# A Mamba block on one core: the seam columns of u*B move from GpSimd to VectorE and ScalarE

## The chip, the cores and the metric

The kernel runs on one core of a Trainium2 chip. The metric is the device time of one execution in microseconds. TensorE is called PE, VectorE DVE, ScalarE ACT, GpSimd POOL and SyncE SP, as the profile does.

## The reference, cut to what matters

The input has 2 sequences of 2048 rows and 512 columns. A layer norm with modulation stands ahead of a Mamba mixer (1024 channels, 16 states a channel), and a second layer norm with modulation ahead of one dense layer that stands for the sum of 8 factors; each branch is gated and added to the input. The change is in the mixer's recurrence, which is elementwise over channels and states and sequential over rows:

```
dA  = exp(dt[..., None] * A)
dBu = (dt * h)[..., None] * Bp[:, :, None, :]
s   = s * dA_t + dBu_t            # one step for each of the 2048 rows
y   = einsum('lben,bln->ble', states, Cp) + h * D
```

In the kernel's names, `u` is dt*h, `ub` is u*B, `decay` is dA, and the product of the states with C is summed over the 16 states by PE.

## The kernel before, in words

All data is fp32. Rows are taken in 16 chunks of 256 rows, 8 for each sequence. The 1024 channels are 8 tiles of 128 partitions, taken as 4 pairs. A **unit** is one of the 16 states for one pair of tiles: 128 partitions by 2*256 columns. So a chunk has 64 units. A **quad** is 4 units (16 quads in a chunk, 4 for each pair of tiles), a **step** is 2 units (32 in a chunk, called s).

For each unit, ACT writes the decays (an exp, two instructions of 256 and 255 columns, `decays`, L722) into one of three PSUM banks. DVE scans them with `ub` (L1426): a unit's 512 columns are scanned in one instruction, although its two halves belong to two tiles. The scan of the first half must not run on into the second, so the decay at the seam (the first column of the second half) is zero (ACT writes that zero, L718, where the product with C overwrote it), and the state that the second tile carries in from the chunk before is added to `ub` in that one column instead. The value that is added is seam = exp(decay rate * dt of the row) * carried state, 128 x 4 for a quad. Chunks 0 and 8 begin a sequence and have no such value; the other 14 do, and are called seamed here.

POOL makes `ub` for a quad at a time (`make_ub`, L568: 128 x 2048 columns out of `u` and `b_all`), two quads ahead of the scans, in a ring of three. In a seamed chunk it then waits for its own product and adds 4 seam values to it (L582); twice a chunk it multiplies the exps (made by ACT, `seam_decays`, L845) with the carried states (`make_seam`, L554).

The states are multiplied with C in one of two places. For each quad a table (`EVEN_POOL`, `ODD_POOL` for chunks 2 to 14, by their parity) says how many of its 4 units, the last ones, go to POOL: DVE scans these into `state_p` in SBUF and POOL multiplies them in one instruction (`multiply_c`, L596, 128 x 512 or 128 x 1024 columns). The other units stay in their PSUM bank, and DVE multiplies them into `sc_d` (L1441). After that, ACT copies the last column to `carry` (`keep_carry`, L706). PE turns every product by a matmul with the identity and sums it in one bank (L1010).

Beside this, every chunk has other work, put at written-out steps on every engine: projections, taps and gates of the neighbouring chunks on PE; `taps` (L1481), `silu_before`, `silu_gate`, residual sums and statistics on DVE; modulation, tanh, copies and softplus on ACT; `u` (L545) and two small norm steps on POOL. Every engine works its own list in order, and semaphores tie the lists together. POOL's order at quad q is: make `ub` of quad q+2 (which waits for the scans of quad q-1), then the product with C of quad q (which waits for the scans of quad q and for the carry copy of its last unit), then `u` at quads 0, 2, 3 and 13. SP's list holds the loads; the load of B for a chunk waits for the last quads of `ub` of the chunk before.

Where data lies matters for the rows below. `decay`, `bank_a`, `bank_c` and `y_bank` are PSUM banks; `ub`, `u`, `b_all`, `c_all`, `state_p`, `sc_d`, `seam`, `carry`, `hc`, `dt`, `yg`, `xc`, `bias_row` and the rest are in SBUF. A scan has one tensor input in PSUM (the decays) and one in SBUF (`ub`), and so has DVE's product with C.

Of the kernel before, what the change touches and what calls it, by code (L numbers as in the profile page):

```python
# [22 lines left out]
ALU = mybir.AluOpType  # L23
# [12 lines left out]
PAIRS = KE // 2  # L36
UNITS = N * PAIRS
# [20 lines left out]
EVEN_POOL = (2, 2, 2, 2, 2, 2, 2, 2, 2, 2, 2, 1, 1, 1, 1, 1)  # L58
ODD_POOL = (2, 2, 2, 2, 1, 2, 2, 2, 2, 2, 2, 1, 1, 1, 1, 1)
# [17 lines left out]
NORMS = 2 + LB  # L77

# [38 lines left out]
def seam_count(c):  # L117

    return c - c // PER

# [44 lines left out]
def build(nc, x, win_m, xp_t, dt_t, wo_t, chan, cond_t, wmod, factors, bias, out):  # L165
# [11 lines left out]
    with ExitStack() as ctx:  # L177
# [83 lines left out]
        ub_product, seam_decay, seam_made, seam_zeroed = sem("ub_product"), sem("seam_decay"), sem("seam_made"), sem("seam_zeroed")  # L261
# [60 lines left out]
        def _(sp):  # L322
# [10 lines left out]
            def load_b(c, par, h):  # L333

                if c:
                    sp.wait_ge(ub_made, QUADS * c - 2 * (1 - h) - 1)
                sp.wait_ge(bc_stored, 16 * c + 16)
# [175 lines left out]
        def _(pool):  # L513
# [33 lines left out]
            def make_seam(c, half):  # L547

                qs = slice(2 * half, 2 * half + 2)
                pool.wait_ge(seam_decay, 2 * seam_count(c) - 1 + half)  # L550
                pool.wait_ge(carried, carries_after(UNITS * (c - 1) + N * qs.stop - 1))
                odd = carry[c // PER][:, :, :].rearrange("p n (q j) -> p n q j", j=2)[:, :, qs, 1]
                part = seam[c % 2][:, :, qs]
                pool.tensor_tensor(part, part, odd, ALU.mult).then_inc(seam_made, 1)  # L554

            def make_ub(quad):
# [7 lines left out]
                if q == 0 and n % (N // 2) == 0 or quad == 1:  # L564
# [6 lines left out]
                                   ALU.mult).then_inc(ub_product if c % PER else ub_made, 1)  # L571
                if c % PER == 0:
                    return
                if g == 0:
                    make_seam(c, 0)
                    pool.wait_ge(seam_made, 2 * seam_count(c) - 1)
                if g == 4:
                    make_seam(c, 1)
                    pool.wait_ge(seam_made, 2 * seam_count(c))
                pool.wait_ge(ub_product, QUADS * (seam_count(c) - 1) + g + 1)  # L580
                first = ub[:, slot, :, 1, 0]
                pool.tensor_tensor(first, first, seam[c % 2][:, n:n + QUAD, q], ALU.add).then_inc(ub_made, 1)  # L582
# [107 lines left out]
        def _(act):  # L690
# [146 lines left out]

            def seam_decays(c, par, half):
# [78 lines left out]
            def one_round(c, par, la, lc):  # L917
                for s in range(STEPS):
# [22 lines left out]
                    if c == 0 and s in (7, 12):  # L941
                        rows_absolute(s // 12, (0.5, RANK ** -0.5)[s // 12])
# [787 lines left out]
```

## Time and profile before

| | |
|---|---|
| median of 3 runs | 2019.82 us (2019.42 to 2027.12) |
| the profiled execution | 2025.55 us, its span 2023.8 us |
| PE matmul | 1759.7 us busy, 87% of the span |
| DVE | 1867.4 us, 92% |
| ACT | 1517.1 us, 75% |
| POOL | 1835.7 us, 91% |
| mean granted PE clock | 0.973 |

How to read it: the busy time is what an engine's own instructions took, the time an instruction needed to get at its operands included, but not the time for which it was held back by a semaphore. The span is some microseconds short of the device time. The chain that ended last passes through PE (42% of the span), ACT (19%), POOL (15%) and DVE (13%).

### The profile page before, as it was taken

To read this page: it belongs to the slowest core of one execution; us is meant where nothing else is said; L and a number is where in the kernel's file an instruction comes from. 1 tells how busy PE (TensorE), PEld (TensorE's weight loads), DVE (VectorE), ACT (ScalarE), POOL (GpSimd) and SP (SyncE) were. 2 spreads that over 40 slices of the span, in tenths; PEclk is the share of its full clock that TensorE was granted. 3 is DMA by queue.
4 is the path that set the end of the run, shared out by engine and by line. 5 is a ranking of instruction groups with operands and counts; after the bars stand their busy time and mean duration, and the time that the engine had idled before them with its cause. 6 is when DMAs were issued, how large, how long until landed. Compare 5 with 4: busy or idle time off the path is not lost.

```text
span 2023.8 us, 29343 instructions
## 1 busy us (share of the span) xinstructions
PE 1759.7 (87%) x9128; PEld 1312.2 (65%) x9128; DVE 1867.4 (92%) x2240; ACT 1517.1 (75%) x4646; POOL 1835.7 (91%) x925
## 2 busy tenths in 40 slices
PE   7985889889889898988989888898988899898798
PEld 5664757667576765757666675766757576676564
DVE  2799989999999999999999999999999999999995
ACT  3767778697877869777786977878787786878662
POOL 1789999999999999999998999999999999999992
PEclk9897999999999999999999999999999999999798
DMA  4656514132140412304042240403223040311200
GB/s 171 235 114 153 140 48 147 31 121 79 43 143 15 152 47 97 103 30 154 17 141 68 111 141 22 157 22 131 68 73 121 28 156 22 121 53 55 92 27 32
DMA packets 72001, 186.17 MB, mean 92 GB/s; under 512 B 6818, under 2 KB 8482, under 8 KB 63908
## 3 DMA queue, kind: packets, MB, share of 16 engines
q1 hardware_dynamic: 68148, 176.95, 26.3%
q0 software_dynamic: 3696, 7.34, 2.2%
q8 instruction: 73, 1.20, 0.2%
q14 instruction: 84, 0.69, 0.1%
HBM read 172.20 MB, written 12.06 MB: 91 GB/s over the span
## 4 chain that ended last, share of the span: by engine, by line
PE 42%; ACT 19%; POOL 15%; DVE 13%; issue 9%; DMA 1%; DVEq 0%; POOLq 0%; SPq 0%; ACTq 0%
PE y_bank L1010 10%; PE bank_a L1085 10%; PE bank_c L1157 9%; POOL ub L568 8%; ACT decay L722 7%; DVE decay L1426 5%; POOL state_p L596 5%; PE bank_c L1057 4%; DVE state_p L1426 3%; PE bank_a L1068 2%; ACT dt L835 2%; DVE sc_d L1441 2%; ACT L722 2%; ACT hT L737 2%; ACT L835 2%
## 5 line engine op out<-in xcount | busy, mean ns | idle before, releaser
L568 POOL TENSOR_TENSOR ub<-u,b_all 128x2048 f32<-128x2048 f32 x255 | 1160.4, 4551 | 48.5 <-DMA b_all<-bc_scratch 47.4
L722 ACT ACTIVATE decay<-dt,decay_rate 128x256 f32<-128x256 f32 (+1 forms) x2048 | 889.6, 466 | 36.0 <-DVE state_p L1426 34.3
L1426 DVE TENSOR_TENSOR_SCAN decay<-decay,carry,ub 128x512 f32<-128x512 f32 x610 | 763.7, 1277 | 25.8 <-ACT decay L722 23.8
L596 POOL TENSOR_TENSOR state_p<-state_p,c_all 128x1024 f32<-128x1024 f32 (+1 forms) x256 | 498.7, 1948 | 85.3 <-ACT carry L706 82.4
L1426 DVE TENSOR_TENSOR_SCAN state_p<-decay,carry,ub 128x512 f32<-128x512 f32 x414 | 527.4, 1274 | 9.3 <-ACT decay L722 7.2
L1010 PE MATMUL y_bank<-ident,sc_d 128*128 128x128 f32 x2440 | 362.5, 283 | 79.9 <-DVE sc_d L1441 79.5
L1441 DVE TENSOR_TENSOR sc_d<-decay,c_all 128x512 f32<-128x512 f32 x610 | 406.7, 671 | 0.0
L1010 PEld LDWEIGHTS y_bank<-ident,sc_d 128*128 128x128 f32 x2440 | 292.9, 145 | 146.1 <-DVE sc_d L1441 120.8
L706 ACT ACTIVATE carry<-decay 128x2 f32<-128x2 f32 x610 | 100.8, 165 | 264.8 <-DVE sc_d L1441 262.9
L1010 PEld LDWEIGHTS y_bank<-ident,state_p 128*128 128x128 f32 x1656 | 195.7, 143 | 126.9 <-POOL state_p L596 71.7
L1010 PE MATMUL y_bank<-ident,state_p 128*128 128x128 f32 x1656 | 231.0, 279 | 53.2 <-POOL state_p L596 52.0
L1085 PE MATMUL bank_a<-hT,win_h 128*128 128x256 f32 x992 | 240.5, 387 | 32.4 <-DVE hc L1490 30.0
L1057 PE MATMUL bank_c<-hT,win_z 128*128 128x256 f32 x960 | 230.7, 387 | 0.0
L1157 PE MATMUL bank_c<-wo,yg 128*128 128x512 f32 x480 | 223.8, 594 | 0.0
L1085 PEld LDWEIGHTS bank_a<-hT,win_h 128*128 128x128 f32 x992 | 182.3, 193 | 58.7 <-DVE hc L1490 35.7
L1057 PEld LDWEIGHTS bank_c<-hT,win_z 128*128 128x128 f32 x960 | 181.7, 196 | 22.6
L1068 PE MATMUL bank_a<-pre_z,tap_diag 128*128 128x256 f32 x496 | 120.4, 386 | 12.2 <-DVE bank_a L1481 12.2
L1157 PEld LDWEIGHTS bank_c<-wo,yg 128*128 128x128 f32 x480 | 86.6, 191 | 67.0 <-issue 64.8
L1068 PEld LDWEIGHTS bank_a<-pre_z,tap_diag 128*128 128x128 f32 x496 | 92.7, 191 | 39.8 <-DVE bank_a L1481 15.8
L1187 PE MATMUL bank_c<-ffn,hT 128*128 128x512 f32 x240 | 115.9, 605 | 0.0
L1001 PE MATMUL y_bank<-ident,skipped 128*128 128x128 f32 x256 | 42.9, 294 | 71.5 <-ACT y_rows L811 71.5
L718 ACT ACTIVATE decay<-ident 128x1 f32<-128x1 f32 x608 | 103.4, 170 | 0.1
(139 smaller groups left out, 1842.1 us busy)
## 6 DMA issues: line engine op xcount, KB each, us to landing
win_h<-win_m SPq DMA_DIRECT2D x128, 256.0 KB, 2.6
win_z<-win_m SPq DMA_DIRECT2D x128, 256.0 KB, 2.8
b_all<-bc_scratch SPq DMA_DIRECT2D x31, 1024.0 KB, 4.7
c_all<-bc_scratch SPq DMA_DIRECT2D x31, 1024.0 KB, 6.6
xa<-x SPq DMA_DIRECT2D x16, 512.0 KB, 5.0
xc<-x SPq DMA_DIRECT2D x16, 512.0 KB, 3.8
out<-xc SPq DMA_DIRECT2D x15, 512.0 KB, 4.0
ffn<-factors POOLq DMA_DIRECT2D x7, 1024.0 KB, 10.0
```

The source lines that it names most:

```text
L568: pool.tensor_tensor(ub[:, slot, :, :, :], u[:, (PAIRS * c + q) % U_PAIRS, :, :].unsqueeze(1).to_broadcast([P, QUAD, 2, ROWS]), b_all[:, n ...
L596: pool.tensor_tensor(part, part, c_all[:, n + QUAD - k:n + QUAD, :].unsqueeze(2).to_broadcast([P, k, 2, ROWS]), ALU.mult).then_inc(pooled, 1)
L718: act.activation(bk[:, ROWS:ROWS + 1], ident[:, 0:1], ACT.Copy, scale=0.0)
L722: last = act.activation(bk[:, j * ROWS + j:(j + 1) * ROWS], dt[:, pair % DT_PAIRS, j, j:], ACT.Exp, scale=decay_rate[:, e, n:n + 1])
L1010: last = pe.matmul(y_bank[:, at:at + P], tile[:, j, t * P:(t + 1) * P], ident[:, :], start=False, stop=last_of_pair, is_transpose=True, sk ...
L1057: last = pe.matmul(dst[:, j * ROWS:(j + 1) * ROWS], tile[:, k, :], hTc[:, k, :], start=(k == 0), stop=(k == KD - 1))
L1068: last = pe.matmul(h_lane(c, q)[:, j * ROWS:(j + 1) * ROWS], tap_diag[:, i, 2 * q + j, :], pre[q % 2][:, j, k:k + ROWS], start=False, stop ...
L1085: last = pe.matmul(h_lane(c, q)[:, j * ROWS:(j + 1) * ROWS], win_h[i % H_TILES][:, k, :], hT[c % H_RING][:, k, :], start=(k == 0 and j == ...
L1157: last = pe.matmul(bank_c[t][:, :], yg[:, k, t * P:(t + 1) * P], wo[:, k, :], start=(k == 0), stop=(k == KE - 1))
L1187: last = pe.matmul(bank_c[t][:, :], hT[c % H_RING][:, k, t * P:(t + 1) * P], ffn[:, k, :], start=False, stop=(k == KD - 1))
L1426: dve.tensor_tensor_scan(dst, bk[:, :], ub[:, quad % UB_RING, i, :, :].rearrange("p j r -> p (j r)"), carried_in[:, n, 2 * q:2 * q + 1], A ...
L1441: dve.tensor_tensor(sc_d[:, i % D_RING, :, :], bk[:, :].rearrange("p (j r) -> p j r", j=2), c_all[:, n:n + 1, :].to_broadcast([P, 2, ROWS] ...
```

## The change

Four parts; the first three concern the 14 seamed chunks:

- POOL no longer touches the seam: `make_seam`, the wait for its own product and the small sum L582 go. `make_ub` raises `ub_made` at once.
- DVE makes the whole seam column ahead. `carry_seam` (two a chunk, 128 x 32 columns) does what `make_seam` did. `add_to_seam` (five a chunk, 128 x 16 or 128 x 8 columns) adds u*B of the seam's row to it, from `b_all`, `u` (as the per-partition scalar) and `seam`. In the chunk's own steps they stand at s = 1, 4, 5, 12 and 20, and for the next chunk at s = 28 and 29, each behind `scan(unit)` and ahead of `scan(unit + 1)` of that step.
- ACT copies 4 values from `seam` over the column in `ub` (`add_seam`, 16 a chunk), ahead of the decays of each quad's first unit; it waits for `ub_made` and `seam_added`. DVE's scan of a quad's first unit waits for that copy (`ub_seamed`). On ACT `tanh_gate` moves ahead of other work of its step at s = 1, 3, 5.
- The tables: in chunks 2 to 14 quads 11 and 13 give two products to POOL instead of one, quad 7 gives one instead of two, and in the odd ones quad 4 gives two instead of one. POOL then has 28 products in each of these chunks, against 27 (even) and 26 (odd). SP's load of B also waits for `seam_added`.

```diff
-EVEN_POOL = (2, 2, 2, 2, 2, 2, 2, 2, 2, 2, 2, 1, 1, 1, 1, 1)
-ODD_POOL = (2, 2, 2, 2, 1, 2, 2, 2, 2, 2, 2, 1, 1, 1, 1, 1)
+EVEN_POOL = (2, 2, 2, 2, 2, 2, 2, 1, 2, 2, 2, 2, 1, 2, 1, 1)
+ODD_POOL = (2, 2, 2, 2, 2, 2, 2, 1, 2, 2, 2, 2, 1, 2, 1, 1)
...
+SEAM_ADDS = PAIRS + 1
...
                 if c:
                     sp.wait_ge(ub_made, QUADS * c - 2 * (1 - h) - 1)
+                    wait(sp, seam_added, SEAM_ADDS * seam_count(c - 1))
...
-            def make_seam(c, half):
...
-                                   ALU.mult).then_inc(ub_product if c % PER else ub_made, 1)
-                if c % PER == 0:
-                    return
-                if g == 0:
-                    make_seam(c, 0)
-                    pool.wait_ge(seam_made, 2 * seam_count(c) - 1)
-                if g == 4:
-                    make_seam(c, 1)
-                    pool.wait_ge(seam_made, 2 * seam_count(c))
-                pool.wait_ge(ub_product, QUADS * (seam_count(c) - 1) + g + 1)
-                first = ub[:, slot, :, 1, 0]
-                pool.tensor_tensor(first, first, seam[c % 2][:, n:n + QUAD, q], ALU.add).then_inc(ub_made, 1)
+                                   ALU.mult).then_inc(ub_made, 1)
...
+            def add_seam(quad):
+
+                c, g = quad // QUADS, quad % QUADS
+                q, n = QUAD * g // N, QUAD * g % N
+                act.wait_ge(ub_made, quad)
+                act.wait_ge(seam_added, SEAM_ADDS * (seam_count(c) - 1) + (q + 1 if q or n >= N // 2 else 0) + 1)
+                act.activation(ub[:, quad % UB_RING, :, 1, 0], seam[c % 2][:, n:n + QUAD, q], ACT.Copy).then_inc(ub_seamed, 1)
...
+                    if c % PER and s % 2 == 0:
+                        add_seam(step // 2)
                     decays(2 * step)
...
+                elif i == 0 and quad // QUADS % PER:
+                    dve.wait_ge(ub_seamed, seamed_count(quad))
...
+            def carry_seam(c, half):
+
+                qs = slice(2 * half, 2 * half + 2)
+                dve.wait_ge(seam_decay, 2 * seam_count(c) - 1 + half)
+                dve.wait_ge(carried, carries_after(UNITS * (c - 1) + N * qs.stop - 1))
+                odd = carry[c // PER][:, :, :].rearrange("p n (q j) -> p n q j", j=2)[:, :, qs, 1]
+                part = seam[c % 2][:, :, qs]
+                dve.tensor_tensor(part, part, odd, ALU.mult).then_inc(seam_made, 1)
+
+            def add_to_seam(c, q, half=None):
+
+                pair = PAIRS * c + q
+                ns = slice(0, N) if half is None else slice(half * N // 2, (half + 1) * N // 2)
+                dve.wait_ge(u_made, pair)
+                dve.wait_ge(seam_made, 2 * seam_count(c) - 1 + q // 2)
+                if q == 0:
+                    dve.wait_ge(b_loaded[half], 16 * c + 16)
+                part = seam[c % 2][:, ns, q]
+                dve.scalar_tensor_tensor(out=part, in0=b_all[:, ns, 0], scalar=u[:, pair % U_PAIRS, 1, 0:1], in1=part,
+                                         op0=ALU.mult, op1=ALU.add).then_inc(seam_added, 1)
...
+                    if c % PER and s == 1:
+                        add_to_seam(c, 0, 1)
+                    if c % PER and s == 4:
+                        carry_seam(c, 1)
+                    if c % PER and s in (5, 12, 20):
+                        add_to_seam(c, {5: 1, 12: 2, 20: 3}[s])
+                    if la is not None and (c + 1) % PER and s == 28:
+                        carry_seam(c + 1, 0)
+                    if la is not None and (c + 1) % PER and s == 29:
+                        add_to_seam(c + 1, 0, 0)
                     scan(unit + 1)
```

## Rows read from the trace of the kernel before

**Rows 1.** The page: busy us, share of the span and instructions of each engine.

```profile
PE 1759.7 (87%) x9128; PEld 1312.2 (65%) x9128; DVE 1867.4 (92%) x2240; ACT 1517.1 (75%) x4646; POOL 1835.7 (91%) x925
```

**Rows 2.** Windows, one stretch of a chunk's length: PE, PEld, DVE, ACT, POOL, clock, DMA.

```profile
600.00:720.00 120.00, 106.37 (x566) 80.30 (x565) 114.55 (x138) 93.96 (x288) 115.34 (x59) 0.99 0.26 84
```

**Rows 3.** Groups by form: line, engine, out<-in, count | busy us, mean ns | idle before.

```profile
L568 POOL TENSOR_TENSOR ub<-u,b_all 128x2048 f32<-128x2048 f32 x255 | 1160.4, 4551 | 48.5 <-DMA b_all<-bc_scratch 47.4
...
L1441 DVE TENSOR_TENSOR sc_d<-decay,c_all 128x512 f32<-128x512 f32 x610 | 406.7, 671 | 0.0
L596 POOL TENSOR_TENSOR state_p<-state_p,c_all 128x1024 f32<-128x1024 f32 x158 | 372.8, 2359 | 66.4 <-ACT carry L706 63.5 <-DVE decay L1426 2.7
...
L596 POOL TENSOR_TENSOR state_p<-state_p,c_all 128x512 f32<-128x512 f32 x98 | 126.0, 1285 | 18.9 <-ACT carry L706 18.9
...
L582 POOL TENSOR_TENSOR ub<-ub,seam 128x4 f32<-128x4 f32 x224 | 46.8, 209 | 17.6
...
L706 ACT ACTIVATE carry<-state_p 128x4 f32<-128x4 f32 x158 | 30.8, 195 | 0.5 <-DVE state_p L1426 0.5
```

**Rows 4.** The same view, DVE alone: its operations whose two tensor inputs are in SBUF.

```profile
L1544 DVE SCALAR_TENSOR_TENSOR bias_row<-bias_row,dt 2x512 f32<-2x512 f32 x1 | 10.3, 10256 | 0.0
...
L1573 DVE TENSOR_TENSOR u<-dt,hc 128x512 f32<-128x512 f32 x1 | 0.7, 693 | 7.1 <-ACT dt L835 7.1
...
L1584 DVE SCALAR_TENSOR_TENSOR cond_s<-cond_s,cond 128x8 f32<-128x8 f32 x1 | 0.2, 168 | 3.6 <-ACT cond_s L898 3.6
```

**Rows 5.** Timeline around L1544 (POOL and DVE): start us, us, engine, operation.

```profile
145.64 2.83 POOL L618 TENSOR_TENSOR wo<-wo,y_rows 128x1024 f32<-128x1024 f32 x1
...
146.73 10.26 DVE L1544 SCALAR_TENSOR_TENSOR bias_row<-bias_row,dt 2x512 f32<-2x512 f32 x1
...
147.96 4.96 POOL L568 TENSOR_TENSOR ub<-u,b_all 128x2048 f32<-128x2048 f32 x1
152.43 1.71 POOL L596 TENSOR_TENSOR state_p<-state_p,c_all 128x512 f32<-128x512 f32 x1
153.65 2.78 POOL L611 TENSOR_TENSOR hT<-wo,y_rows 128x1024 f32<-128x1024 f32 x1
...
156.51 2.68 POOL L618 TENSOR_TENSOR wo<-wo,y_rows 128x1024 f32<-128x1024 f32 x1
156.91 1.27 DVE L1426 TENSOR_TENSOR_SCAN decay<-decay,carry,ub 128x512 f32<-128x512 f32 x1
```

**Rows 6.** Timeline, POOL then DVE, around step 4 of chunk 4.

```profile
575.93 4.54 POOL L568 TENSOR_TENSOR ub<-u,b_all 128x2048 f32<-128x2048 f32 x1
...
580.70 2.36 POOL L596 TENSOR_TENSOR state_p<-state_p,c_all 128x1024 f32<-128x1024 f32 x1
583.00 4.55 POOL L568 TENSOR_TENSOR ub<-u,b_all 128x2048 f32<-128x2048 f32 x1
...
577.43 2.46 DVE L1426 TENSOR_TENSOR_SCAN decay<-decay,carry,ub 128x512 f32<-128x512 f32 x2
```

**Rows 7.** Timeline, POOL then DVE, steps 1 and 2 of chunk 4.

```profile
566.68 4.53 POOL L568 TENSOR_TENSOR ub<-u,b_all 128x2048 f32<-128x2048 f32 x1
...
572.37 2.36 POOL L596 TENSOR_TENSOR state_p<-state_p,c_all 128x1024 f32<-128x1024 f32 x1 [0.87 <-ACT carry L706]
...
568.98 1.27 DVE L1426 TENSOR_TENSOR_SCAN state_p<-decay,carry,ub 128x512 f32<-128x512 f32 x1
...
570.75 2.65 DVE L1426 TENSOR_TENSOR_SCAN decay<-decay,carry,ub 128x512 f32<-128x512 f32 x2
```

**Rows 8.** Timeline, POOL then DVE, around step 28 of chunk 4.

```profile
670.00 1.27 POOL L596 TENSOR_TENSOR state_p<-state_p,c_all 128x512 f32<-128x512 f32 x1
671.23 1.28 POOL L545 TENSOR_TENSOR u<-dt,hc 128x512 f32<-128x512 f32 x1
672.59 4.54 POOL L568 TENSOR_TENSOR ub<-u,b_all 128x2048 f32<-128x2048 f32 x1
...
669.51 1.28 DVE L1426 TENSOR_TENSOR_SCAN decay<-decay,carry,ub 128x512 f32<-128x512 f32 x1
```

More of the change, by code:

```diff
@@ L119, in seam_count, with seamed_count @@
     return c - c // PER
+def seamed_count(quad):
+    c, g = quad // QUADS, quad % QUADS
+    return QUADS * (seam_count(c) - 1) + g + 1
 def products_after(unit):
@@ L260, in build @@
         skip_turned, y_copied = sem("skip_turned"), sem("y_copied")
-        ub_product, seam_decay, seam_made, seam_zeroed = sem("ub_product"), sem("seam_decay"), sem("seam_made"), sem("seam_zeroed")
+        ub_seamed, seam_decay, seam_made, seam_zeroed = sem("ub_seamed"), sem("seam_decay"), sem("seam_made"), sem("seam_zeroed")
+        seam_added = sem("seam_added")
         a_full = [sem(f"a_full{i}") for i in range(2)]
@@ L545, in make_u @@
                 pool.tensor_tensor(u[:, pair % U_PAIRS, :, :], dt[:, pair % DT_PAIRS, :, :], hc[:, k, :], ALU.mult).then_inc(u_made, 1)
-            def make_seam(c, half):
[L549 to L554, printed above, removed]
             def make_ub(quad):
@@ L836, in soft_dt @@
                 last.then_inc(dt_made, 1)
+            def add_seam(quad):
+                c, g = quad // QUADS, quad % QUADS
+                q, n = QUAD * g // N, QUAD * g % N
+                act.wait_ge(ub_made, quad)
+                act.wait_ge(seam_added, SEAM_ADDS * (seam_count(c) - 1) + (q + 1 if q or n >= N // 2 else 0) + 1)
+                act.activation(ub[:, quad % UB_RING, :, 1, 0], seam[c % 2][:, n:n + QUAD, q], ACT.Copy).then_inc(ub_seamed, 1)
             def seam_decays(c, par, half):
                 act.wait_ge(dt_made, PAIRS * c + 2 * half + 2)
-                wait(act, ub_made, QUADS * (c - 1) - 1)
+                wait(act, ub_seamed, QUADS * seam_count(c - 2))
                 for q in (2 * half, 2 * half + 1):
@@ L942, in one_round @@
                         rows_absolute(s // 12, (0.5, RANK ** -0.5)[s // 12])
+                    if lc is not None and s in (1, 3, 5):
+                        tanh_gate(c - 1, {1: 1, 3: 2, 5: 3}[s])
                     if s in (4, 6, 12):
@@ L962, in one_round @@
                     if lc is not None:
-                        if s in (1, 3, 5):
-                            tanh_gate(c - 1, {1: 1, 3: 2, 5: 3}[s])
                         if s == 21:
```

## The prediction, made before the changed kernel was run

> **What bounds the kernel now.** I read the page first: DVE is busy for 1867 us and POOL for 1836 us of the span, ACT for 1517 us [rows 1]. Then the windows, to see whether that is an average over unlike stages. It is not: one stretch of 120 us in the middle has DVE at 114.6 us and POOL at 115.3 us, ACT at 94 us and PE at 106 us at almost its full clock [rows 2]. DVE has 5.4 us in such a stretch in which it is not busy. So DVE is the engine that hardly ever rests, POOL is close behind, and any time that DVE loses beyond 5.4 us a chunk is lost to the kernel. Next the groups by form, for prices: a product with C takes DVE 0.671 us and POOL 1.29 us for one unit or 2.36 us for two, a quad of `ub` takes POOL 4.55 us, the seam sum 0.209 us, and a carry copy of 4 columns takes ACT 0.195 us [rows 3].
>
> **What a small operation on DVE costs.** The change puts 7 of them into each of 14 chunks, 98 in all: 2 `carry_seam` and 5 `add_to_seam`. By width they should be cheap: one of 8 columns took 0.168 us [rows 4]. But they differ from DVE's daily work in one thing. Scans and products with C have one tensor input in PSUM; each of the seven has both in SBUF. So I looked for DVE operations of that kind in the trace. There are three. Two took 0.168 and 0.693 us, as their widths ask, and both ran before POOL began its first `ub`. The third, L1544, 512 columns wide like the one of 0.693 us, took 10.256 us [rows 4].
>
> The timeline shows what it did in that time: nothing, as long as POOL ran [rows 5]. It starts at 146.73, when POOL is in L618. POOL goes on through `ub`, a product and L611, its instructions following each other without a hole. L611 ends at 156.43, the next POOL instruction waits for L611's own result and starts at 156.51, and in this hole of 0.08 us DVE gets in: it ends at 156.99, 0.56 us after L611, its plain duration. POOL's next instruction is 0.3 us longer than others of 1024 columns (2.68 against 2.36 us [rows 3, 5]). So a DVE operation with two SBUF inputs is shut out while POOL runs, and once shut out it waited through three of POOL's instruction boundaries. It is one case, but one of one.
>
> The Trainium skill, SBUF — State Buffer, section Who interferes with whom, has the rule: a DVE instruction with two SBUF inputs contends with a GpSimd instruction that reads SBUF, whoever starts first has the shared ports for its whole instruction, and the other fully blocks. The trace agrees that DVE blocks; it goes further than the rule in that three boundaries passed.
>
> **The sum of the stalls.** DVE works in order, so scans and products queue behind the shut-out instruction, and ACT's decays, which wait for freed banks, behind these. What ends a stall is POOL running dry: at quad q it makes `ub` of quad q+2 and then needs the scans of quad q, which DVE now withholds. So a stall lasts from the insertion to the end of `ub` of quad q+2, unless POOL has a hole earlier.
> - Step 4 (quad 2). Chunk 4 starts that quad's first two scans at 577.43 and the operation would stand between them, at about 578.66. POOL starts the product of quad 1 at 580.70 and ends `ub` of quad 4 at 587.55 [rows 6]. As it stands that is 8.9 us. But stalls let POOL catch up. The least that it can lag is seen where it waited for the carry copy: product at 572.37, first scan of the next quad at 570.75, a lag of 1.62 us [rows 7], in place of 3.27. Then the stall is 1.62 + 6.85 (product to end of `ub`) - 1.23 = 7.2 us. I take the least lag, since the stalls recur. The operation of step 5 finds POOL waiting and costs nothing.
> - Steps 12 and 20 (quads 6 and 10) have the same pattern: 7.2 us each, 8.9 at most.
> - Step 1: DVE is at 568.98, POOL in a `ub` until 571.21 and then without work: 2.2 us [rows 7].
> - Step 28: DVE is at 669.51; POOL has the product of quad 13 ahead, which the new table makes 1.1 us longer, and then `u`, ending at 672.51. The `ub` behind needs that `u`, and there is a hole of 0.08 us [rows 8]. So 3.0 + 1.1 = 4.1 us. Step 29 costs 0 to 1 us.
>
> Together 21.6 + 2.2 + 4.1 = 28 us a chunk, 34 with POOL's present lag. The 5.4 us that DVE now waits [rows 2] partly vanish, since during a stall PE and ACT catch up; I take 4. That leaves 24 us a chunk and, for 14 chunks, 336 us. The last value is an estimate; the bound below is a stall of nothing but the operation itself (98 times 0.17 = 17 us), and I take the blocked value because it is the row of the same kind of operands that decides.
>
> **The other terms.** DVE loses 19 products with C (7 even chunks with one, 6 odd with two): 19 * 0.67 = 13 us less, against 17 us for the seven operations' own time. POOL loses 224 sums and 28 products of the seam, each with a wait of its own, and gains 19 products of 1.07 us each; it will be the one that waits, so this is worth nothing. ACT gets 224 copies of 0.195 us [rows 3], 3.1 us a chunk, and has 26 us free [rows 2], more when DVE is late; nothing. `add_seam` waits for POOL's `ub` ahead of the decays. At quad 4 of chunk 4 that `ub` ends at 587.55 and POOL is to be ahead of the scans more than now, so this wait is nothing while DVE is late. Moving `tanh_gate` is worth tenths of a microsecond. SP's added wait is for additions of the chunk before, long done. So the rest sums to about zero.
>
> The sum is made against the profiled execution: 2025.55 + 336 = 2361. The median lies 5.7 us lower, so the forecast is **2355 us**. With the slack used in full and stalls of 24 us a chunk it is some 2270, with POOL's present lag and 2 us of slack regained some 2470: its own range.
>
> **Rivals.**
> - *Taking turns* (0.18): the shared ports change hands at each boundary, and a stall is only what is left of POOL's current instruction. Speaking for it: L1544 is one case. Against it: L1544 itself. At step 4 DVE would wait from 578.66 for a `ub` that ends at 580.47, 1.8 us [rows 6]; at step 1, 2.2 us [rows 7]; taken as 1.8 us for each of the seven it is 12.6 us, less 4 to 5 of slack, so 7.5 us a chunk: 105 us, **2125 us**. This is what the page's rule gives by its letter (The Trainium skill, SBUF — State Buffer).
> - *No shutting out* (0.12), the other side: operations of 8 to 32 columns slip in, and L1544 was late for another reason, its 2 partitions or its DMA-loaded input. Place: the late quads, 11 and 13, where DVE and ACT are both full. Price: the 19 products with C are gained, at most 13 us, POOL's relief helps in chunk 1, where it has extra work, some 3 us, and the own time is half hidden. That is -8 us, **2012 us**. It decides if a seam operation takes DVE under 0.3 us on average.
> - *ACT becomes the bound* (0.04): shutting out does not occur, and the copies lengthen ACT's full stretches. 5 copies a chunk exposed, at 0.2 to 0.3 us, give 14 * 1.3 = 18 us, **2030 to 2040 us**.
> - *More than blocked* (0.04): the stalls make PE idle, its granted clock falls, and its backlog bounds the chunk: over 2470 us.
> - That the change doesn't do what it says: the added operations are unconditional in the seamed chunks, so I give it no chance of its own.
>
> **How the numbers follow.** Blocked with a long stall 0.62, taking turns 0.18, not shut out 0.12, ACT 0.04, worse 0.04. A measurement of this kernel tells about 0.5% (10 us) from no change. The rival at 2012 is split between within 0.5% and faster by more (0.06 and 0.06); ACT's goes to slower but for 0.01; so faster 0.06, same 0.07, slower 0.87. The range reaches from the take-turns case to near the end of the forecast's own: 2110 to 2450; it leaves out the two cases at no change and the worst end, 2 in 10.
>
> **What would show it.** The new DVE groups, 28 and 70 instructions, should have a mean of several microseconds, with the longest at 7 us and those of steps 5 and 29 near 0.2 us, and 300 to 400 us busy in all; each should end about 0.1 to 0.2 us behind a POOL instruction. DVE's share stays over 90%, as a blocked instruction counts as busy; POOL's falls to about 80% with a wait for `carried` ahead of products; ACT's longest wait is for DVE. If those groups' means are under 0.3 us the forecast is wrong altogether; if they are near 2 us the turns are taken and the step that failed is the one that lets a stall run to POOL's running dry.

## The result, and the profile after

The changed kernel takes 2147.09 us (median of 4 runs, 2138.94 to 2147.9), the kernel before 2019.96 us beside it: a ratio of 1.061 [1.058, 1.065], slower by 127 us. The profiled execution is one of these runs, 2147.07 us with a span of 2145.3 us; its mean granted TensorE clock is 0.953, against 0.973 before. (Of the experiments below, the one with an input from PSUM was profiled in a disturbed execution with a span of 4589.6 us, in which POOL was busy for only 39% of the time, so of its rows only single operations of DVE are read, beside what POOL did at that moment.)

The page's line of busy times and the same 120 us stretch as before, after [rows 1] and [rows 2]:

```profile
PE 1806.1 (84%) x9128; PEld 1331.8 (62%) x9128; DVE 2010.9 (94%) x2319; ACT 1532.0 (71%) x4832; POOL 1806.2 (84%) x673
```

```profile
600.00:720.00 120.00, 104.83 (x551) 77.65 (x549) 116.81 (x136) 89.50 (x281) 104.32 (x37) 0.98 0.25 83
```

The forecast was 2355 us. The change is slower, as forecast, but by 127 us and not by 336.

DVE has 143.5 us more of busy time and the span grew by 121.5 us; so DVE's time without work shrank by only 22 us in all, 1.6 us a seamed chunk. In the stretch POOL fell from 115.3 to 104.3 us and ACT from 94 to 89.5: both now wait. Where DVE's time went stands in its groups by form (line, operation, out<-in, count | busy us, mean ns | idle before):

```profile
L1463 DVE TENSOR_TENSOR sc_d<-decay,c_all 128x512 f32<-128x512 f32 x591 | 391.3, 666 | 0.0
L1449 DVE SCALAR_TENSOR_TENSOR seam<-b_all,u,seam 128x16 f32<-128x16 f32 x42 | 70.9, 1689 | 0.0
...
L1449 DVE SCALAR_TENSOR_TENSOR seam<-b_all,u,seam 128x8 f32<-128x8 f32 x28 | 50.0, 1787 | 0.0
L1438 DVE TENSOR_TENSOR seam<-seam,carry 128x32 f32<-128x32 f32 x28 | 45.1, 1611 | 0.0
```

The 98 new operations are busy for 166.0 us (70.9 + 50.0 + 45.1), 1.7 us each where their widths ask for 0.17. The products with C went from 406.7 us [rows 3] to 391.3, the 19 fewer. The two lines by themselves, with the shortest, the median and the longest duration in ns:

```profile
L1438 DVE TENSOR_TENSOR seam<-seam,carry x28: 477/1650/8768, 184.2 to 2012.6; 128x32 f32<-128x32 f32 x28
```

```profile
L1449 DVE SCALAR_TENSOR_TENSOR seam<-b_all,u,seam x70: 218/1524/3477, 192.4 to 2071.8; 128x16 f32<-128x16 f32 x42, 128x8 f32<-128x8 f32 x28
```

The same operation takes 0.5 or 8.8 us, so the price is not the operation's own. The timeline of chunk 4 shows its seven, at steps 1, 4, 5, 12, 20, 28 and 29 (start us, duration us):

```profile
603.90 0.35 DVE L1449 SCALAR_TENSOR_TENSOR seam<-b_all,u,seam 128x8 f32<-128x8 f32 x1
...
614.64 1.88 DVE L1438 TENSOR_TENSOR seam<-seam,carry 128x32 f32<-128x32 f32 x1
...
619.99 3.32 DVE L1449 SCALAR_TENSOR_TENSOR seam<-b_all,u,seam 128x16 f32<-128x16 f32 x1
...
650.36 0.32 DVE L1449 SCALAR_TENSOR_TENSOR seam<-b_all,u,seam 128x16 f32<-128x16 f32 x1
...
681.22 1.52 DVE L1449 SCALAR_TENSOR_TENSOR seam<-b_all,u,seam 128x16 f32<-128x16 f32 x1
...
710.21 0.50 DVE L1438 TENSOR_TENSOR seam<-seam,carry 128x32 f32<-128x32 f32 x1
...
715.39 3.47 DVE L1449 SCALAR_TENSOR_TENSOR seam<-b_all,u,seam 128x8 f32<-128x8 f32 x1
```

And POOL's timeline in the same stretches:

```profile
611.92 4.54 POOL L568 TENSOR_TENSOR ub<-u,b_all 128x2048 f32<-128x2048 f32 x1
616.42 2.35 POOL L585 TENSOR_TENSOR state_p<-state_p,c_all 128x1024 f32<-128x1024 f32 x1
618.74 4.53 POOL L568 TENSOR_TENSOR ub<-u,b_all 128x2048 f32<-128x2048 f32 x1
...
678.16 4.53 POOL L568 TENSOR_TENSOR ub<-u,b_all 128x2048 f32<-128x2048 f32 x1
...
714.28 4.54 POOL L568 TENSOR_TENSOR ub<-u,b_all 128x2048 f32<-128x2048 f32 x1
```

Step 4's operation starts in a `ub` that ends at 616.46 and ends itself at 616.52. Step 5's ends at 623.31, the `ub` at 623.27; step 20's at 682.74, the `ub` at 682.69; step 29's at 718.86, the `ub` at 718.82. Each ends 0.04 to 0.06 us behind the end of the POOL instruction that was under way when it came, and POOL's next one, though ready (the product at 616.42), does not keep it out. That is a stall of what is left of one instruction. The two timelines read in full say the same of nearly all: 95 of the 98 end 0.02 to 0.06 us behind the end of the one POOL instruction under way, and in 42 of these POOL's next instruction followed without a hole. Two more found POOL without work (231.40 and 2043.93) and took 0.23 and 0.22 us. Over the 14 seamed chunks the mean is 0.47 us at step 1, 2.28 at step 4, 3.11 at step 5, 0.37 at step 12, 1.59 at step 20, 0.94 at step 28 and 3.10 at step 29, 11.9 us a chunk.

There is one exception, step 4 of chunk 1. DVE, then POOL (the first of POOL's rows lies ahead of the stall):

```profile
219.15 8.77 DVE L1438 TENSOR_TENSOR seam<-seam,carry 128x32 f32<-128x32 f32 x1
```

```profile
215.25 1.29 POOL L592 DMA_DIRECT2D ffn<-factors  x1
216.07 5.04 POOL L568 TENSOR_TENSOR ub<-u,b_all 128x2048 f32<-128x2048 f32 x1
220.57 2.84 POOL L585 TENSOR_TENSOR state_p<-state_p,c_all 128x1024 f32<-128x1024 f32 x1
222.88 4.97 POOL L568 TENSOR_TENSOR ub<-u,b_all 128x2048 f32<-128x2048 f32 x1
```

Here DVE waits through three POOL instructions, to 227.92, and the first of them follows a DMA that POOL issues. The same was ahead of L1544 in the kernel before, the single case on which the prediction built. The rows ahead of [rows 5], the timeline of POOL in the kernel before:

```profile
143.62 1.26 POOL L596 TENSOR_TENSOR state_p<-state_p,c_all 128x512 f32<-128x512 f32 x1
144.82 1.26 POOL L603 DMA_DIRECT2D ffn<-factors  x1
```

The waits of POOL, from the page, show that POOL in turn waits for what DVE is late with:

```profile
L585 POOL TENSOR_TENSOR state_p<-state_p,c_all 128x1024 f32<-128x1024 f32 (+1 forms) x256 | 519.7, 2030 | 253.9 <-ACT carry L695 233.4
```

Ahead of its products POOL waits 233.4 us for carry copies, against 82.4 before (63.5 + 18.9 [rows 3]). Those copies wait for DVE.

### The profile page after: what moved, and what is told of

Same layout as the page of the kernel before. It is cut to its first block and busy times, and to the rows that moved or that the text cites. A ratio compares the mean times of both kernels' runs of the same rounds, so it can differ in the third digit from the quotient of the medians.

```text
span 2145.3 us, 29601 instructions
## 1 busy us (share of the span) xinstructions
PE 1806.1 (84%) x9128; PEld 1331.8 (62%) x9128; DVE 2010.9 (94%) x2319; ACT 1532.0 (71%) x4832; POOL 1806.2 (84%) x673
## 5 line engine op out<-in xcount | busy, mean ns | idle before, releaser
L1427 DVE TENSOR_TENSOR_SCAN decay<-decay,carry,ub 128x512 f32<-128x512 f32 x591 | 739.8, 1273 | 26.1 <-ACT decay L711 25.7
L585 POOL TENSOR_TENSOR state_p<-state_p,c_all 128x1024 f32<-128x1024 f32 (+1 forms) x256 | 519.7, 2030 | 253.9 <-ACT carry L695 233.4
L1427 DVE TENSOR_TENSOR_SCAN state_p<-decay,carry,ub 128x512 f32<-128x512 f32 x433 | 549.9, 1270 | 15.2 <-ACT decay L711 14.3
L1009 PEld LDWEIGHTS y_bank<-ident,sc_d 128*128 128x128 f32 x2364 | 280.9, 145 | 242.0 <-DVE sc_d L1463 218.5
L1463 DVE TENSOR_TENSOR sc_d<-decay,c_all 128x512 f32<-128x512 f32 x591 | 391.3, 666 | 0.0
L1009 PEld LDWEIGHTS y_bank<-ident,state_p 128*128 128x128 f32 x1732 | 208.5, 145 | 100.2 <-issue 50.0
L1009 PE MATMUL y_bank<-ident,state_p 128*128 128x128 f32 x1732 | 242.4, 281 | 25.0 <-POOL state_p L585 25.0
L1056 PE MATMUL bank_c<-hT,win_z 128*128 128x256 f32 x960 | 246.3, 406 | 0.0
L1067 PE MATMUL bank_a<-pre_z,tap_diag 128*128 128x256 f32 x496 | 132.2, 414 | 21.9 <-DVE bank_a L1503 21.1
L1449 DVE SCALAR_TENSOR_TENSOR seam<-b_all,u,seam 128x16 f32<-128x16 f32 (+1 forms) x70 | 121.0, 1728 | 0.0
```

The source lines that it names most:

```text
L585: pool.tensor_tensor(part, part, c_all[:, n + QUAD - k:n + QUAD, :].unsqueeze(2).to_broadcast([P, k, 2, ROWS]), ALU.mult).then_inc(pooled, 1)
L1009: last = pe.matmul(y_bank[:, at:at + P], tile[:, j, t * P:(t + 1) * P], ident[:, :], start=False, stop=last_of_pair, is_transpose=True, sk ...
L1056: last = pe.matmul(dst[:, j * ROWS:(j + 1) * ROWS], tile[:, k, :], hTc[:, k, :], start=(k == 0), stop=(k == KD - 1))
L1067: last = pe.matmul(h_lane(c, q)[:, j * ROWS:(j + 1) * ROWS], tap_diag[:, i, 2 * q + j, :], pre[q % 2][:, j, k:k + ROWS], start=False, stop ...
L1427: dve.tensor_tensor_scan(dst, bk[:, :], ub[:, quad % UB_RING, i, :, :].rearrange("p j r -> p (j r)"), carried_in[:, n, 2 * q:2 * q + 1], A ...
L1449: dve.scalar_tensor_tensor(out=part, in0=b_all[:, ns, 0], scalar=u[:, pair % U_PAIRS, 1, 0:1], in1=part, op0=ALU.mult, op1=ALU.add).then_i ...
```

## The experiments

Three questions: is it where the inputs lie, what ends a stall, and what is the rest of the change worth. Each run is compared with the kernel before on its own chip; where times of two chips are subtracted, the ratios give the same within 3 us.

### Is it the two SBUF inputs?

The first try gives each of the seven operations one tensor input from SBUF. It leaves out the product with the carried states and the sum.

```diff
-                dve.tensor_tensor(part, part, odd, ALU.mult).then_inc(seam_made, 1)
+                dve.tensor_scalar(part, part, 1.0, None, ALU.mult).then_inc(seam_made, 1)
...
-                dve.scalar_tensor_tensor(out=part, in0=b_all[:, ns, 0], scalar=u[:, pair % U_PAIRS, 1, 0:1], in1=part,
-                                         op0=ALU.mult, op1=ALU.add).then_inc(seam_added, 1)
+                dve.tensor_scalar(part, b_all[:, ns, 0], u[:, pair % U_PAIRS, 1, 0:1], None, ALU.mult).then_inc(seam_added, 1)
```

> The seven seam operations a chunk stay on DVE, at their steps and with their waits, but each reads only one tensor in SBUF (the product with the carried state and the sum are left out). Theory ports (a DVE operation with two SBUF inputs waits for the POOL instruction under way): both groups fall from 1.6 and 1.7 us to about 0.2 us each, 166 us of them become 20, and the kernel returns to 2005 to 2025 us. Theory small operations (their strides, widths or waits cost the time): the groups keep a mean over 1 us and the kernel stays over 2120 us. Theory copies and tables (ACT's copies or the new tables cost the time): the groups fall, but the kernel stays over 2080 us.

2143.48 us, ratio 1.059 [1.056, 1.061]: nothing gained, and the theory of the ports, as I had written it, missed; the run came out as "small operations" said. The means are those of the change within 11 ns:

```profile
L1449 DVE TENSOR_SCALAR seam<-b_all,u 128x16 f32<-128x16 f32 x42 | 71.0, 1691 | 0.0
...
L1449 DVE TENSOR_SCALAR seam<-b_all,u 128x8 f32<-128x8 f32 x28 | 50.3, 1798 | 0.0
L1438 DVE TENSOR_SCALAR seam<-seam 128x32 f32<-128x32 f32 x28 | 45.1, 1611 | 0.0
```

So "two SBUF inputs" is not the whole condition. The form was badly chosen to tell the theories apart: an operation from SBUF to SBUF with one input of even width waits as well. In the same profile the one-column `tensor_scalar` of the norms keeps its 0.197 us. The Trainium skill has a reason, in SBUF — State Buffer, section Who interferes with whom: `tensor_scalar` can use both ports for one tensor and then contends too. By VectorE: DVE Perf Modes of the Trainium skill, section Mode 2×_2P — use both read ports for one tensor, this wants SBUF and an outermost dimension that is even, or odd and the same in input and output. The rows agree with it and do not prove it.

The next replaces them by an operation that reads the same columns of `b_all` and `carry` and writes 6 statistics elsewhere. What is added to `ub` is then the exp alone.

```diff
-                dve.tensor_tensor(part, part, odd, ALU.mult).then_inc(seam_made, 1)
+                dve.bn_stats(seam_stat[:, 0, :], carry[c // PER][:, :, 2 * half + 1]).then_inc(seam_made, 1)
...
-                dve.scalar_tensor_tensor(out=part, in0=b_all[:, ns, 0], scalar=u[:, pair % U_PAIRS, 1, 0:1], in1=part,
-                                         op0=ALU.mult, op1=ALU.add).then_inc(seam_added, 1)
+                dve.bn_stats(seam_stat[:, 1, :], b_all[:, ns, 0]).then_inc(seam_added, 1)
```

> The seven seam operations a chunk on DVE are replaced, at their steps and with their waits, by row statistics over the same columns, an operation with one SBUF input that ran unhindered beside POOL 62 times in the kernel before (the product with the carried state and the sum are left out). Theory ports, now: a DVE operation waits for the POOL instruction under way if it reads SBUF through both interfaces, with two inputs or with one input in a form that is read in two halves, as the one-input form of the first experiment may be. Then these take about 0.2 us each, 20 us in all, and the kernel returns to 2005 to 2030 us. Theory small operations (widths, strides or waits): they keep the pattern of 0.4, 1.9, 3.3, 0.3, 1.5, 0.5 and 3.5 us by step, and the kernel stays over 2120 us.

```profile
L1450 DVE BATCH_NORM_STATS2 seam_stat<-b_all 128x6 f32<-128x16 f32 x42 | 7.2, 172 | 0.0
...
L1439 DVE BATCH_NORM_STATS2 seam_stat<-carry 128x6 f32<-128x16 f32 x28 | 4.8, 172 | 0.0
```

2024.60 us, ratio 1.001 [1.000, 1.002], as the theory now said. All 98 take 16.6 us in place of 166 (the 28 of 8 columns 4.6 us of it), and 83 of them begin and end inside a POOL instruction that goes on. The kernel is back at its old time. With the places, waits, copies and tables of the change all kept, 119 us (2143.48 - 2024.60) hang on the kind of operation and where it writes. This rules out every theory by which an added DVE instruction, a wait or an ACT copy costs the time. That the two engines share a way into SBUF is an inference; the runs show which operations wait, and for what.

A third keeps the real operations but takes one input of those at steps 4, 12, 20 and 28 from PSUM, the bank of the unit just scanned (so the values are not the seam's).

```diff
-                dve.tensor_tensor(part, part, odd, ALU.mult).then_inc(seam_made, 1)
+                dve.wait_ge(scanned, unit + 1)
+                bk = decay[bank_of[unit]][:, 0:2 * N].rearrange("p (n q) -> p n q", q=2)
+                dve.tensor_tensor(part, part, bk, ALU.mult).then_inc(seam_made, 1)
...
+                    dve.wait_ge(scanned, unit + 1)
+                    other = decay[bank_of[unit]][:, 0:N]
```

> The changed kernel; at steps 4, 12, 20 and 28 the seam operation, same operation and same columns, takes its second input from a PSUM bank (a decay bank, so the value is not the carried state or the running sum). Steps 1, 5 and 29 are as they were. Theory ports: the operations of steps 4, 12, 20 and 28 take 0.15 to 0.3 us at each of those steps and no longer end behind a POOL instruction; the other three still do, with 2 to 4 us at step 5 and 29. The time falls by 30 to 70 us, to 2080 to 2115. Theory small operations: nothing changes, 2140 to 2155 us.

```profile
L1455 DVE SCALAR_TENSOR_TENSOR seam<-b_all,u,seam 128x16 f32<-128x16 f32 x14 | 53.7, 3838 | 0.0
...
L1455 DVE SCALAR_TENSOR_TENSOR seam<-b_all,u,decay 128x16 f32<-128x16 f32 x28 | 6.8, 244 | 2.2 <-issue 0.3
...
L1440 DVE TENSOR_TENSOR seam<-seam,decay 128x32 f32<-128x32 f32 x28 | 5.3, 189 | 2.0
```

2074.68 us, ratio 1.025 [1.024, 1.027]. The means by themselves would not do, since POOL is often idle in this profile. But 28 of the 56 with a PSUM input lie inside a POOL instruction, and none of them waits for its end; all 14 of step 5, with both inputs in SBUF, do. One of the 28, DVE and then POOL:

```profile
557.93 0.25 DVE L1455 SCALAR_TENSOR_TENSOR seam<-b_all,u,decay 128x16 f32<-128x16 f32 x1
```

```profile
555.29 4.50 POOL L568 TENSOR_TENSOR ub<-u,b_all 128x2048 f32<-128x2048 f32 x1
```

It is through at 558.18, 1.61 us before the `ub` ends. So the same instruction at the same width takes 0.25 us beside POOL with a PSUM input, and 3.84 us with both in SBUF. The time is 5 us below the range that I had expected; 72 of the 127 us are gone with 56 of the 98 stalls, which in the change were 5.2 of the 11.9 us a chunk, 73 us in all.

### What ends a stall?

Doubling: ahead of each operation one of the same kind, into a buffer that nobody reads.

```diff
+                dve.tensor_tensor(seam_twice[:, 0, :, :], odd, odd, ALU.mult)
                 dve.tensor_tensor(part, part, odd, ALU.mult).then_inc(seam_made, 1)
...
+                dve.scalar_tensor_tensor(out=seam_twice[:, 1, ns, 0], in0=b_all[:, ns, 0], scalar=u[:, pair % U_PAIRS, 1, 0:1], in1=b_all[:, ns, 1],
+                                         op0=ALU.mult, op1=ALU.add)
```

> The changed kernel with a second operation of the same kind and columns right ahead of each of the seven, into a scratch tile. Theory turns (the interface is given for one whole instruction, and POOL's next instruction has it by the time the first DVE operation is through): the second of each couple waits for a whole further POOL instruction, 1.2 to 4.5 us, so the groups together take 300 to 450 us and the kernel 2250 to 2400 us. Theory hole (DVE is only kept out at the start and then runs on): the second costs 0.1 to 0.2 us, 14 us in all, and the kernel takes 2155 to 2170 us.

2225.45 us, ratio 1.100 [1.098, 1.103], below the 2250 us that I had expected at least: only 43 of the 98 second operations are shut out again (1.3 us or more), and the other 55, under 0.3 us, found no POOL instruction under way. DVE and then POOL, at steps 4 and 5 of chunk 4:

```profile
626.55 1.45 DVE L1439 TENSOR_TENSOR seam_twice<-carry 128x32 f32<-128x32 f32 x1
627.92 2.38 DVE L1440 TENSOR_TENSOR seam<-seam,carry 128x32 f32<-128x32 f32 x1
...
633.77 1.00 DVE L1451 SCALAR_TENSOR_TENSOR seam_twice<-b_all,u 128x16 f32<-128x16 f32 x1
634.70 0.24 DVE L1453 SCALAR_TENSOR_TENSOR seam<-b_all,u,seam 128x16 f32<-128x16 f32 x1
```

```profile
623.40 4.54 POOL L569 TENSOR_TENSOR ub<-u,b_all 128x2048 f32<-128x2048 f32 x1
627.89 2.36 POOL L586 TENSOR_TENSOR state_p<-state_p,c_all 128x1024 f32<-128x1024 f32 x1
630.21 4.53 POOL L569 TENSOR_TENSOR ub<-u,b_all 128x2048 f32<-128x2048 f32 x1
638.36 2.36 POOL L586 TENSOR_TENSOR state_p<-state_p,c_all 128x1024 f32<-128x1024 f32 x1 [3.63 <-ACT carry L696]
```

The first ends at 628.00, behind the `ub` (627.94). The second waits out the product that was next in line and ends at 630.30, behind 630.25. At 634.7 POOL has no work for 3.63 us, and the second takes its plain 0.24 us. Turns are taken instruction by instruction.

Is it the width? The kernel before gets, at steps 12 and 20 of chunks 1 to 14, a product of two SBUF tensors of 160 columns (odd chunks) or 64 (even), that nobody reads.

```diff
+                dve.tensor_tensor(wide[:, 0:width], flat[:, 0, 0:width], flat[:, 1, 0:width], ALU.mult)
...
+                    if 1 <= c < CHUNKS - 1 and s in (12, 20):
+                        wide_product(160 if c % 2 else 64)
```

> The kernel before with one DVE product of two SBUF inputs (constants, into a scratch tile) added at steps 12 and 20 of chunks 1 to 14, 160 columns wide in the odd chunks and 64 in the even ones. It is to tell why the operation of 512 columns in chunk 0 stayed out over three POOL boundaries. Theory width (a wide operation does not fit between two POOL instructions): those of 160 columns stay out over more than one boundary, 5 us or more, those of 64 columns end at the first. Theory overlap (it is POOL's instructions that follow each other closer behind a POOL DMA issue): both widths end at the first boundary, 0.1 and 0.2 us behind it, outside chunk 1. Time 2035 to 2060 us with overlap, over 2080 us with width.

```profile
247.93 0.40 DVE L1435 TENSOR_TENSOR wide<-tap_diag 128x160 f32<-128x160 f32 x1
```

```profile
245.78 2.36 POOL L629 TENSOR_TENSOR hT<-ffn,xc 128x1024 f32<-128x1024 f32 x1
248.10 4.62 POOL L569 TENSOR_TENSOR ub<-u,b_all 128x2048 f32<-128x2048 f32 x1
```

2068.23 us, ratio 1.022 [1.020, 1.025], 8 us above the 2060 that I had put for "overlap". The products take 1.3 us on average, so the stall is seen without anything else of the change, and on constants that POOL does not read at that time. None of the 28 goes past a boundary, the longest of 160 columns takes 3.76 us and the longest of 64 takes 1.95. That is weaker than it looks: 5 found POOL without work, and 20 met a hole of 0.07 to 0.09 us at the boundary, where the kernel before waits for its `ub` ahead of the seam's sum. Only three came to a boundary without a hole, two of 64 columns and the one of 160 shown, which comes while L629 is under way and ends at 248.33, 0.19 us behind it, though the `ub` follows at once. So nothing here speaks for width as the cause of L1544's long stall, but 512 columns were not tried.

The DMA that POOL issued ahead of both long stalls is what was left. This puts one (64 KB from SBUF, read by nobody) behind quad 0's product in four chunks of the changed kernel, so that it lies ahead of step 4.

```diff
+                    if c in (3, 5, 11, 13) and g == 0:
+                        pool.dma_start(ident_dram[(3, 5, 11, 13).index(c)], ident[:, :]).then_inc(ident_stored, 16)
```

> The changed kernel with one more DMA issued by POOL (64 KB of the identity into a scratch buffer) after the product of quad 0 in chunks 3, 5, 11 and 13, as in chunk 1, where the operation of step 4 took 8.8 us. Theory overlap (behind a DMA issue POOL's instructions follow each other so closely that DVE gets in at none of their boundaries until POOL has to wait): in these four chunks the operation of step 4 takes 6 to 9 us, with POOL's instructions recorded 0.4 to 0.5 us ahead of the end of the one before, and 1.9 us in the other chunks; the kernel takes 10 to 30 us more than the changed one, 2155 to 2175 us. Theory chance (chunk 1 was special by POOL's lag alone): 1 to 3 us in all chunks but chunk 1.

2175.15 us, ratio 1.076 [1.074, 1.078]. DVE and POOL in chunk 3, step 4:

```profile
480.19 9.30 DVE L1443 TENSOR_TENSOR seam<-seam,carry 128x32 f32<-128x32 f32 x1
```

```profile
477.48 0.65 POOL L661 DMA_DIRECT2D ident_scratch<-ident  x1
478.15 4.55 POOL L571 TENSOR_TENSOR ub<-u,b_all 128x2048 f32<-128x2048 f32 x1
482.65 2.34 POOL L588 TENSOR_TENSOR state_p<-state_p,c_all 128x1024 f32<-128x1024 f32 x1
484.96 4.48 POOL L571 TENSOR_TENSOR ub<-u,b_all 128x2048 f32<-128x2048 f32 x1
```

In all four chunks step 4's operation takes 9.25 to 9.30 us: DVE is passed over at 482.7 and 485.0 and gets in at 489.44, when POOL has to wait for a carry copy that DVE holds up. In chunk 1 it is 8.79 us, as in the change, and in the other nine chunks 0.95 to 1.89. So the stall to POOL's running dry exists, but behind a DMA that POOL issued, and an operation of 32 columns is enough for it. The theory of overlap was right on this and wrong on the sign it named: POOL's rows overlap here by 0.05 us (478.15 + 4.55 against 482.65), as everywhere, and not by the 0.5 us of chunk 1.

The changed kernel's own trace has the counter-case, step 28 of chunk 0. DVE, then POOL:

```profile
184.24 4.05 DVE L1438 TENSOR_TENSOR seam<-seam,carry 128x32 f32<-128x32 f32 x1
```

```profile
180.97 1.77 POOL L592 DMA_DIRECT2D ffn<-factors  x1
181.79 1.18 POOL L540 TENSOR_TENSOR nrm_a<-mv_a,small 128x2 f32<-128x2 f32 x1
183.05 0.71 POOL L542 TENSOR_TENSOR nrm_a<-nrm_a,small 128x2 f32<-128x2 f32 x1
183.74 4.49 POOL L568 TENSOR_TENSOR ub<-u,b_all 128x2048 f32<-128x2048 f32 x1
188.20 1.25 POOL L585 TENSOR_TENSOR state_p<-state_p,c_all 128x512 f32<-128x512 f32 x1
```

It also comes 3.3 us behind a DMA issue (in chunk 1 it was 3.9 us), but L542 waits for the result of L540 (a hole from 182.97 to 183.05), and the operation gets in at the next boundary: it ends at 188.29, the `ub` at 188.23. It may be that one wait of POOL's ends the condition, as a hole ended L1544's stall; the two short instructions between the issue and the `ub` are as good a candidate, and no run separates them. Why the issue brings it about, no run shows either.

### What is the rest worth?

```diff
-EVEN_POOL = (2, 2, 2, 2, 2, 2, 2, 1, 2, 2, 2, 2, 1, 2, 1, 1)
-ODD_POOL = (2, 2, 2, 2, 2, 2, 2, 1, 2, 2, 2, 2, 1, 2, 1, 1)
+EVEN_POOL = (2, 2, 2, 2, 2, 2, 2, 2, 2, 2, 2, 1, 1, 1, 1, 1)
+ODD_POOL = (2, 2, 2, 2, 1, 2, 2, 2, 2, 2, 2, 1, 1, 1, 1, 1)
```

The change with the tables of before:

> The changed kernel with the tables of the kernel before. Theory ports: DVE has 19 products more, so 2150 to 2165 us, and the seam operations still take 130 to 200 us in all. Theory tables: 2100 us or less, as the extra POOL products were what cost time.

2153.15 us, ratio 1.064 [1.063, 1.066], 6 us above the change, with intervals that overlap; the seam operations take 146.3 us. Both are as the theory of the ports had them: the tables are not what costs.

The kernel before with the new tables alone (the same lines, the other way round):

> The kernel before with the new tables alone. Theory ports: the tables cost little; POOL gets 19 products of 1.07 us and DVE loses 19 of 0.67 us, 2010 to 2035 us. Theory tables: over 2060 us.

2015.98 us, ratio 0.997 [0.996, 0.998]: the best of all versions, by 0.3%, which is below the 0.5% that I had set as telling, but with an interval that leaves out 1. In its stretch from 600 to 720 us DVE is busy for 113.91 us, against 114.55 [rows 2], and POOL for 115.60, against 115.34: a little of DVE's work handed to the other engine.

That with the tanh also moved ahead, as in the change:

```diff
+                    if lc is not None and s in (1, 3, 5):
+                        tanh_gate(c - 1, {1: 1, 3: 2, 5: 3}[s])
...
-                        if s in (1, 3, 5):
-                            tanh_gate(c - 1, {1: 1, 3: 2, 5: 3}[s])
```

> The kernel before with the new tables and with the gate's tanh moved ahead on ACT, as in the change; nothing of the seam is moved. The tables alone gave 0.9967 of the kernel before. If the move is worth something, 2008 to 2014 us; if not, 2014 to 2018 us.

2021.98 us, ratio 1.000 [0.999, 1.001], outside both ranges of the expectation. With the move the gain of the tables, 0.3%, is gone, where the prediction had the move at tenths of a microsecond; which wait brings that about was not looked for.

Last, the seam made ahead as in the change, but by POOL (each sum with its product as two instructions), with ACT's copies and the new tables:

```diff
+                pool.tensor_tensor(part, part, odd, ALU.mult).then_inc(seam_made, 1)
...
+                pool.tensor_tensor(first, b_all[:, ns, 0], u[:, pair % U_PAIRS, 1, 0:1].to_broadcast([P, first.shape[1]]), ALU.mult).then_inc(seam_times, 1)
...
+                pool.tensor_tensor(part, part, first, ALU.add).then_inc(seam_added, 1)
...
-                dve.tensor_tensor(part, part, odd, ALU.mult).then_inc(seam_made, 1)
...
-                dve.scalar_tensor_tensor(out=part, in0=b_all[:, ns, 0], scalar=u[:, pair % U_PAIRS, 1, 0:1], in1=part,
-                                         op0=ALU.mult, op1=ALU.add).then_inc(seam_added, 1)
```

> The seam columns are made ahead on POOL instead of DVE (two products with the carried state and five times a product and a sum a chunk, 12 small POOL instructions in place of 18 and their waits), ACT copies them in, new tables. Theory ports: no DVE operation with two SBUF inputs is left in the chunks, so 2005 to 2025 us, at best 10 us under the kernel before by the 19 products that DVE no longer makes. Theory copies: ACT's 224 copies with their wait for the ub of POOL hold the decays back, over 2045 us. Theory POOL: POOL with 28 products and the seam becomes the bound, 2025 to 2050 us, with DVE idle behind ub.

2030.1 us, ratio 1.003 [1.002, 1.004]. Off DVE, the scheme costs 0.3% and not 6%; it doesn't pay either. The time lies in the range that I had given for POOL as the bound, and not in the one for the ports alone; whether POOL bounds it is not shown, as the same with the old tables has no result.

## Why the prediction was right on the cause and wrong on its size

- **The sign and the first half of the mechanism held.** That DVE operations with both inputs in SBUF wait for POOL, that scans queue behind them, and that this outweighs every other part was the reason given, and the run with the statistics in their place shows it: 119 us. The size did not hold: 336 us were forecast and 127 measured. That 2147 us lies between 2110 and 2450 is owed to the take-turns rival, down to which the range was stretched; the forecast's own began at 2270.
- **The step that failed** is "What ends a stall is POOL running dry". It made the stalls 28 us a chunk; they are 11.9. A stall runs to the end of the one POOL instruction under way. The trace had one long stall, and I carried its rule over to all places without asking what was special about its own: POOL had issued a DMA 0.8 us before the instruction in which the stall began, a row that stood directly ahead of those I read. With such an issue set ahead of it, the same operation took 9.3 us in place of 1.88.
- **Step 4, forecast 7.2 us**, has 2.28 on average and 1.88 typically, 8.77 in the one chunk where the forecast's condition exists. The term of the rival that takes turns, 1.8 us, was read from the right rows.
- **Step 5, forecast 0, has 3.11, and step 29, forecast 0 to 1, has 3.10.** The first zero hung on the failed step: with the long stall at step 4 POOL would have run dry, and in chunk 1, where it does, step 5 takes 0.23 us. With a short one POOL goes on into its next `ub` (618.74), and step 5 falls into it early. For step 29 the prediction gave no reason. These two are more than half of all stalls.
- **Steps 12 and 20, forecast 7.2 each**, have 0.37 and 1.59: at step 12 of chunk 4 the operation starts 0.28 us before a `ub` ends (646.10 + 4.54). That is luck of the phase, and it repeats: 12 of the 14 chunks have 0.30 to 0.33 there. Steps 1 and 28, forecast 2.2 and 4.1, have 0.47 and 0.94.
- **The slack, taken as 4 us of 5.4**, was too hopeful: 1.6 us a chunk came back. With measured terms the forecast's own sum is 11.9 for the stalls, less 1.1 for the products with C (15.4 us over 14), less 1.6: 9.2 us a chunk, 129 us, against 121.5 of span; the rest of DVE's work is 7.1 us shorter. As the 1.6 is itself taken from the span, this checks that the terms are complete and not what causes them.
- **The take-turns rival (2125 us)** had the right rule. Its sum of stalls, 12.6, is near 11.9 in part by luck, as a flat 1.8 stands for steps of 0.37 to 3.11. It took off 5.1 us of slack where 1.6 came back; the 0.7 too much in the stalls and the 1.1 for the products, which it did not take off, made up for about half of that, hence only 22 us low. The section Who interferes with whom in SBUF — State Buffer of the Trainium skill says it by its letter, with the lock held for a whole instruction; I let one row overrule it, where the row and the rule could both be had by asking what came before the row. I gave it 0.18.
- **The other terms at zero together** held: with the stalls taken out the ratio is 1.001. Singly they did not: the tables gain 0.3%, and with the tanh's move that gain is gone.
- **What was to be seen**: POOL's share near 80% (84%), a longer wait ahead of its products, DVE above 90% (94%). The means "near 2 us", 1.6 to 1.8, were the sign named for the failed step. The operations end 0.02 to 0.06 us behind POOL's instruction, and not 0.1 to 0.2.
- **Two sums of the prediction are a little off**: 8.9 three times, 2.2 and 4.1 are 33 and not 34, and stalls of 24 us with the whole slack of 5.4 come to 2280 and not 2270. Neither touches the forecast.

## What to carry to other kernels

Before a small elementwise operation is moved to VectorE beside a GpSimd that is never idle, look at where its inputs lie. With both in SBUF it cost what was left of GpSimd's current instruction, here 1.7 us for 0.17 us of work, and with 4.5 us instructions on the other side 8 columns cost as much as 16 or 32. One input in PSUM (0.25 us beside a `ub`), or a place at which GpSimd waits (0.22 us), avoided that here. And when a forecast rests on one row, read the instructions ahead of it before it is carried over to other places.

## What was not expected of the hardware

- Behind a DMA issue by GpSimd the turn didn't pass to VectorE at an instruction boundary: 8.8, 9.3 and 10.3 us through two and three boundaries, in six places (L1544, chunk 1, and the four made on purpose). There POOL had not waited since the issue and had its next instruction ready at the boundary. At step 1 of chunk 1 (208.25, behind the issue at 198.10) POOL had not waited either, but had nothing ready at the first boundary, and the stall ended there. In 95 of the change's 98 operations it ended with the instruction under way, 0.02 to 0.06 us behind it.
- A one-input `tensor_scalar` from SBUF to SBUF, 8 to 32 columns, waits as long (1.6 to 1.8 us mean) as the two-input form; statistics over the same columns don't (0.17 us).
- Time lost by DVE was not worth the same everywhere. The change lost 143.5 us of it for 121.5 us of span. The doubled operations add 40.6 us of DVE's busy time (2051.5 against 2010.9) and 75.9 us of span, and the wide products on the kernel before 34 us (1901.5) and 43 us. In step with this the granted clock's mean falls, 0.973, 0.953 and 0.933 for the kernel before, the change and the doubled one, and the same 9128 matmuls are busy for 1759.7, 1806.1 and 1847.7 us. That the lower clock makes the difference was not tried.
